# Eight-sequence decoder layer: the first norm turned by a transposing transfer, and products moved across the border of an iteration

## The chip, the cores and the metric

The kernel runs on one core of a Trainium2 chip. TensorE (PE) multiplies and turns 128 by 128 blocks, VectorE (DVE), ScalarE (ACT) and GpSimd (POOL) do elementwise work, and SyncE (SP) issues every transfer. The time is the device time of one execution in microseconds (us). Three executions of the kernel before are known, and one more with a profile.

## The reference

For 8 sequences of 512 rows by 256 columns, one pre-norm decoder layer:

```python
# x, ctx: (8, 512, 256)
x = x + attn(layernorm(x))
x = x + xattn(layernorm(x), ctx, ctx)
x = x + ffn(layernorm(x))

def attn(x):                       # 16 heads of 16 columns
    z = softmax(x @ W_A.T / 4, axis=rows)          # one weight per row and head
    roll[h, i, j] = z[h, i - j] if j <= i else 0   # a lower Toeplitz matrix per head
    return concat_h(roll[h] @ (x @ W_V.T)[:, h]) @ W_O.T + b_O

def xattn(q, k, v):                # one head of 256, causal
    return softmax(causal((q @ WQ) @ (k @ WK).T / 16)) @ (v @ WV)

def ffn(x):                        # 2 shared experts (128 wide), 16 routed (64 wide), best 2
    comb = weights of the two best of softmax(x @ router_w), zero elsewhere
    return sum_shared(silu(x @ wg) * (x @ wu)) @ wd + sum_e(comb[e] * silu(x @ wg[e]) * (x @ wu[e]) @ wd[e])
```

## The kernel before, in words

Each product is made of three half-precision passes on halves "hi" and "lo" of both operands (`three_passes`, lines 140 to 142). So whatever is turned or produced in fp32 is split: ACT writes hi, DVE writes fp32 minus hi as lo.

The program is a software pipeline of ten iterations, 0 to 9. Iteration `it` does three stages on three sequences: the first norm, softmax and values of sequence `it` (flag `f`), the Toeplitz product, W_O, second norm and cross attention of `it - 1` (flag `m`), and the feed forward of `it - 2` (flag `d`). The flag `n` says that a sequence `it + 1` follows. Iterations 2 and 3 (`c` = 6, 7) also compute context products; 4, 5 and 6 are one loop body and are called the steady ones here; 7 has no `n`, 8 has no `f`, 9 has only `d`. The order on each engine is written out by hand, and semaphores join the engines.

On PE a steady iteration is: router logits (`rows<-w_r,h3T`), softmax product z (`score<-h1T,w_a`), Toeplitz products (`wide<-val,toep`) with half the values (`rows<-w_v,h1T`), eight blocks of `mix` turned, the other values, `comb` turned, then ten gate and up products g0/u0 to g9/u9 (`score<-h3T,w_gu`, `rows<-h3T,w_gu`), each followed some steps later by its `down` (`wide<-w_d,mid`). Among them stand W_O (`rows<-w_o,mixT`), the turned `h2`, the scores, probabilities and attention. After u9 come down 7, eight blocks of `h3` turned, down 8, eight blocks of `h1` of the next sequence turned, down 9. The stretch between down 9 of one iteration and the Toeplitz products of the next is called the border. Turned blocks go to the two PSUM banks `turned`, from which ACT and DVE split them to `h1T`, `h2T`, `h3T`, `mixT` (`part_turned`, lines 630 and 819).

On DVE every gate j is `open_gate` (line 878, and line 884 with the router weights that a transfer repeats over partitions: `comb_rows`, in the tile `stage`) and `pass_gate` (line 892). ACT runs the tanh of a gate (line 678) and the hi part of `mid` (683), POOL the lo part (536). `normalise` is line 809. POOL takes the square root of a variance (528, 531) and adds the bias: `x_bo = x_in + b_o` (543), in a steady iteration just behind mid 1. The Toeplitz matrices of a sequence are loaded from a scratch in memory (`toep`, 2 x 2 MB), `x_in` with 512 KB per sequence.

`wide` is both the sum of the down products and the result of the Toeplitz products, so the latter wait until DVE has moved the sum into `x_out` (line 1069, two instructions, one signal).

## Time and profile before

| | |
|---|---|
| median of 3 runs | 645.68 us (642.64 to 646.45) |
| profiled execution | 646.66 us |
| its span in the trace | 644.9 us |
| mean granted TensorE clock | 0.974 of full speed |
| a steady iteration | 66.5 us |

The span is what the trace shows from the first to the last instruction; the profiled execution's own time holds 1.8 us more, which lie around it.

### The profile page before, as it was taken

How to read it: one execution, taken by the hardware profiler on the slowest of the kernel's cores; microseconds unless marked ns; L12 is line 12 of the kernel's file. 1: busy time of each engine (PE TensorE's matmuls, PEld its weight loads, DVE VectorE, ACT ScalarE, POOL GpSimd, SP SyncE). 2: the span in 40 equal slices, each digit the busy share in tenths (PEclk: the TensorE clock that was granted, in tenths of full speed). 3: DMA queues.
4: the chain of work that ended last, by engine and by line, in shares of the span. 5: the costliest groups of instructions: out<-in, count | busy, mean ns of one | idle time of the engine just before them, and what ended most of it. 6: DMA issues, size and time to landing. Idle time of an engine off the chain costs nothing. (4 is left out here: it accounts for less than half of the span.)

```text
span 644.9 us, 13750 instructions
## 1 busy us (share of the span) xinstructions
PE 578.3 (90%) x5212; PEld 388.5 (60%) x5212; DVE 459.1 (71%) x1137; ACT 224.2 (35%) x450; POOL 195.1 (30%) x221
## 2 busy tenths in 40 slices
PE   2768697989999999999999999999989979997696
PEld 1446365755686566766685667666855666664354
DVE  4485567676976788777877797779786866687363
ACT  3564343434243333333333333332423322322121
POOL 4314230332422322243324242414242312132122
PEclk9979789999999999999999999999999998999899
DMA  7884924296116901292119411951186105000600
GB/s 246 284 268 149 343 78 183 76 277 211 67 35 150 343 4 66 79 291 93 67 45 277 138 65 37 240 183 65 37 183 212 67 34 134 1 1 34 132 2 34
DMA packets 61249, 84.26 MB, mean 131 GB/s; under 512 B 2832, under 2 KB 46736, under 8 KB 60944
## 3 DMA queue, kind: packets, MB, share of 16 engines
q1 hardware_dynamic: 61200, 83.60, 43.6%
q8 instruction: 32, 0.52, 0.4%
q14 instruction: 17, 0.14, 0.1%
HBM read 71.47 MB, written 12.12 MB: 130 GB/s over the span
## 5 line engine op out<-in xcount | busy, mean ns | idle before, releaser
L536 POOL TENSOR_TENSOR mid<-gated,mid 128x512 f16<-128x512 f32 x80 | 93.4, 1167 | 233.3 <-ACT mid L683 233.3
L683 ACT ACTIVATE mid<-gated 128x512 f16<-128x512 f32 x80 | 50.1, 627 | 125.6 <-DVEq L895 125.6
L140 PE MATMUL wide<-w_d,mid 128*128 128x256 f16 x320 | 87.9, 275 | 3.5 <-POOL mid L536 3.5
L878 DVE SCALAR_TENSOR_TENSOR gated<-gated,score 128x512 f32<-128x512 f32 x80 | 54.3, 679 | 47.3 <-ACT gated L678 47.3
L141 PE MATMUL wide<-w_d,mid 128*128 128x256 f16 x320 | 87.8, 274 | 0.0
L142 PE MATMUL wide<-w_d,mid 128*128 128x256 f16 x320 | 87.8, 274 | 0.0
L140 PE MATMUL score<-h3T,w_gu 128*128 128x512 f16 x160 | 61.3, 383 | 5.0 <-DVEq L120 3.5
L678 ACT ACTIVATE gated<-score 128x512 f32<-128x512 f32 x80 | 47.2, 590 | 47.5 <-PE score L142 42.6
L140 PE MATMUL rows<-h3T,w_gu 128*128 128x512 f16 x160 | 60.9, 381 | 1.2 <-DVEq L120 1.2
L141 PE MATMUL score<-h3T,w_gu 128*128 128x512 f16 x160 | 61.1, 382 | 0.0
L142 PE MATMUL score<-h3T,w_gu 128*128 128x512 f16 x160 | 61.1, 382 | 0.0
L141 PE MATMUL rows<-h3T,w_gu 128*128 128x512 f16 x160 | 60.9, 380 | 0.0
L142 PE MATMUL rows<-h3T,w_gu 128*128 128x512 f16 x160 | 60.6, 379 | 0.0
L892 DVE SCALAR_TENSOR_TENSOR gated<-gated,rows 128x512 f32<-128x512 f32 x80 | 54.9, 686 | 4.5 <-DVE gated L884 1.0
L884 DVE TENSOR_TENSOR gated<-gated,stage 128x512 f32<-128x512 f32 x64 | 51.0, 797 | 6.8 <-DMA stage<-comb_scratch 4.3
L1099 PE MATMUL turned<-ident,h 128*128 128x128 f32 x192 | 28.4, 292 | 26.3 <-DVE h L809 16.4
L665 ACT ACTIVATE prob<-score,s_bias 128x128 f32<-128x128 f32 (+3 forms) x32 | 16.9, 528 | 78.7 <-DVE s_bias L845 78.7
L140 PE MATMUL wide<-val,toep 128*128 128x64 f16 (+3 forms) x512 | 41.2, 180 | 2.6 <-DVE x_out L1069 1.0
L140 PEld LDWEIGHTS wide<-val,toep 128*128 128x128 f16 x512 | 40.3, 96 | 5.1 <-issue 2.3
L809 DVE TENSOR_SCALAR h<-x_res,mean_var,rstd 128x256 f32<-128x256 f32 x64 | 39.3, 675 | 4.5 <-POOL rstd L531 2.7
L1099 PEld LDWEIGHTS turned<-ident,h 128*128 128x128 f32 x192 | 22.0, 148 | 33.9 <-issue 22.4
L141 PE MATMUL wide<-val,toep 128*128 128x64 f16 (+3 forms) x512 | 41.1, 180 | 0.2 <-issue 0.2
(193 smaller groups left out, 1384.6 us busy)
## 6 DMA issues: line engine op xcount, KB each, us to landing
toep<-z_scratch SPq DMA_DIRECT2D x16, 2048.0 KB, 16.2
stage<-comb_scratch SPq DMA_DIRECT2D x32, 512.0 KB, 8.0
x_in<-in_x SPq DMA_DIRECT2D x8, 512.0 KB, 10.8
out<-x_out SPq DMA_DIRECT2D x8, 512.0 KB, 3.0
qT<-q_scratch SPq DMA_DIRECT2D x7, 512.0 KB, 3.8
vx<-v_scratch SPq DMA_DIRECT2D x7, 512.0 KB, 5.0
q_scratch<-stage SPq DMA_DIRECT2D x6, 512.0 KB, 5.6
v_scratch<-stage SPq DMA_DIRECT2D x6, 512.0 KB, 6.1
```

Of the source, the lines that this page charges most:

```text
L140: pe.matmul(out, stationary[0], moving[0], start=start, stop=False, **kw)
L141: pe.matmul(out, stationary[0], moving[1], start=False, stop=False, **kw)
L142: return pe.matmul(out, stationary[1], moving[0], start=False, stop=stop, **kw)
L536: pool.tensor_tensor(mid[:, 1, j % SLOTS], gated[:, j % SLOTS], mid[:, 0, j % SLOTS], ALU.subtract).then_inc(mid_split.sem, 1)
L665: act.activation(prob[:, c % 2, 0:n], score.bank(f"s{c}")[:, 0:n], ACT.Exp, bias=s_bias[:, c:c + 1], scale=1 / (X_Q * X_H), accum_out=s_su ...
L678: act.activation(gated[:, j % SLOTS], score.bank(f"g{j}")[:], ACT.Tanh, scale=0.5 / (X_H * X_W)).then_inc(tanh_done.sem, 1)
L683: act.activation(mid[:, 0, j % SLOTS], gated[:, j % SLOTS], ACT.Copy).then_inc(mid_hi.sem, 1)
L809: last = dve.tensor_scalar(dst[:, c], src[:, c], mean_var[n][:, c, 0:1], rstd[n][:, c:c + 1], ALU.subtract, ALU.mult)
L878: dve.scalar_tensor_tensor(to, to, 1.0, score.bank(f"g{j}")[:], ALU.add, ALU.mult).then_inc(score.taken.sem, 1)
L884: dve.tensor_tensor(to, to, comb_rows[:, j - NSH], ALU.mult).then_inc(opened.sem, 1)
L892: dve.scalar_tensor_tensor(to, to, X_MID / (2 * (X_H * X_W) ** 2), rows.bank(f"u{j}")[:], ALU.mult, ALU.mult).then_inc(rows.taken.sem, 1)
L1099: last = pe.transpose(turned.bank(f"{use}.{k}")[:, P * c:P * c + P], src[:, c, P * k:P * k + P], ident[:])
```

## The change

1. `h1` of sequences 3 to 7 is no longer turned by PE. `x_in` is loaded from `xr`, a copy of x whose rows run backwards within blocks of 128, and is normalised in place. ACT and DVE split it unturned into `h1p` (hi and lo, 128 x 1024 each), and one transposing DMA of SP writes `h1T`. Sequences 0 to 2 are still turned by PE.
2. At the end of iterations 2 to 6, PE does: u9, h3 turned, down 7, z of the next sequence, down 8, its logits, down 9. The next iteration then begins with the first half of the values, and only then come the Toeplitz products, whose second half waits for the second half of `x_out` alone.
3. `comb` is turned behind g0/u0 and taken by DVE behind gate 0, where both stood ahead of these.
4. `x_bo` is loaded by a transfer of its own (512 KB), and the bias is added in place on POOL at gate 5 instead of gate 1.
5. On DVE, the statistics of the next `x_in` go to gates 3 and 4, its normalisation to gate 5, the new split to gate 6; the third norm stands between opening and passing gate 8; `probT` is split between opening and passing a gate. `h2` and `h3` signal by halves, and PE turns them block row by block row (`turn_halves`).
6. The Toeplitz results lie in `wide` in row order, so that ACT's copy of them (now into `h2`) is no longer permuted.

The core of the diff:

```diff
+            def move_h1(b):
+
+                sp.wait_ge(rows.ready.sem, rows.is_ready(b - 1, "v2"))
+                hold(sp, h1p_split, h1p_split.at(b - 3, 1))
+                sp.dma_start(h1T[:].rearrange("p a k (c s) -> p (a k c) s", s=P),
+                             h1p[:].rearrange("p a k c e -> p (a k c e)"), transpose=True).then_inc(h1T_moved.sem, 16)
...
+                if d and n:
+                    load_x(it + 1, 1 if c == 6 else None)
+                if f and d:
+                    load_residual(it)
...
                 if f and m:
                     fetch_context(it, it)
-                if d:
-                    sp.wait_ge(y_taken.sem, y_taken.at(it - 2, 1))
+                if n and d:
+                    move_h1(it + 1)
+                if d:
+                    sp.wait_ge(y_taken.sem, y_taken.at(it - 2, 2))
...
+            def part_h1(b):
+
+                dve.wait_ge(h1p_hi.sem, h1p_hi.at(b - 3, 1))
+                hi, lo = (h1p[:, a].rearrange("p k c e -> p c k e") for a in range(2))
+                dve.tensor_tensor(lo, x_in[:].rearrange("p c (k e) -> p c k e", k=K2), hi,
+                                  ALU.subtract).then_inc(h1p_split.sem, 1)
...
                 for j in range(AHEAD, MID):
                     if d:
-                        gate(it, it - 2, j)
+                        open_gate(it, it - 2, j)
+                    if m and j == AHEAD + C + 1:
+                        normalise(it - 1, it, 2, x_res, h3)
+                    at = j - AHEAD
+                    if m and at < C:
+                        part_prob(it, it - 1, at)
+                    if d:
+                        pass_gate(it, it - 2, j)
...
-                        if j == 5:
+                        if d and j in (3, 4):
+                            x_statistics(it + 1, range(2 * (j - 3), 2 * (j - 3) + 2))
+                        if first and j == 5:
                             x_statistics(it + 1)
-                        if j == C + AHEAD:
-                            normalise(it + 1, it, 0, x_in, h1)
+                        if j == (5 if d else C + AHEAD):
+                            normalise(it + 1, it, 0, x_in, x_in)
+                        if d and j == 6:
+                            part_h1(it + 1)
...
+            def turn_halves(it, use, src, made, b):
+
+                pe.wait_ge(turned.taken.sem, turned.is_free(it, f"{use}.1"))
+                turned.fill(pe, it, f"{use}.0")
+                turned.reached[(id(pe), True)] = turned.order.index(f"{use}.1") + 1
+                for c in range(C):
+                    if c % 2 == 0:
+                        pe.wait_ge(made.sem, made.at(b, c // 2 + 1))
+                    for k in range(K2):
+                        last = pe.transpose(turned.bank(f"{use}.{k}")[:, P * c:P * c + P], src[:, c, P * k:P * k + P],
+                                            ident[:])
+                        if c == C - 1:
+                            last.then_inc(turned.ready.sem, 1)
...
-                if m:
-                    pe.wait_ge(h_ready[2].sem, h_ready[2].at(it - 1, 1))
-                    turn(it, "h3", h3)
+
+                if d and not m:
+                    down(it - 2, MID - 3)
+                if m:
+                    turn_halves(it, "h3", h3, h_ready[2], it - 1)
+                if d and m:
+                    down(it - 2, MID - 3)
+                if n and d:
+                    score.reach(pe, score.ready, it)
+                    pe.wait_ge(h1T_moved.sem, h1T_moved.at(it - 2, 16))
+                    z_product(it + 1)
+                elif n:
+                    pe.wait_ge(h_ready[0].sem, h_ready[0].at(it + 1, 2))
+                    turn(it, "h1", x_in)
                 if d:
                     down(it - 2, MID - 2)
-                if n:
-                    pe.wait_ge(h_ready[0].sem, h_ready[0].at(it + 1, 1))
-                    turn(it, "h1", h1)
+                if n and d:
+                    turned.reach(pe, turned.ready, it)
+                    rows.reach(pe, rows.ready, it)
+                    logits(it + 1)
                 if d:
                     down(it - 2, MID - 1)
```

How the instructions stand, on VectorE at the end of the loop body (`L878`/`L926` and `L884`/`L932` open a gate, `L892`/`L940` pass it). Before, from gate 7 to the end:

```order
L878 SCALAR_TENSOR_TENSOR gated<-gated,score0 128x512
L884 TENSOR_TENSOR gated<-gated,stage 128x512
L892 SCALAR_TENSOR_TENSOR gated<-gated,rows0 128x512
...
L800 BN_AGGR mean_var2<-stats2 128x2 x4
...
L809 TENSOR_SCALAR h1<-x_in,mean_var0,rstd0 128x256 x4
...
L878 SCALAR_TENSOR_TENSOR gated<-gated,score1 128x512
...
L884 TENSOR_TENSOR gated<-gated,stage 128x512
L892 SCALAR_TENSOR_TENSOR gated<-gated,rows1 128x512
...
L809 TENSOR_SCALAR h3<-x_res,mean_var2,rstd2 128x256 x4
```

And now, from the new split at gate 6:

```order
L859 TENSOR_TENSOR h1p<-x_in,h1p 128x4x2x128
...
L926 SCALAR_TENSOR_TENSOR gated<-gated,score0 128x512
...
L932 TENSOR_TENSOR gated<-gated,stage 128x512
L940 SCALAR_TENSOR_TENSOR gated<-gated,rows0 128x512
...
L833 BN_AGGR mean_var2<-stats2 128x2 x4
...
L926 SCALAR_TENSOR_TENSOR gated<-gated,score1 128x512
...
L932 TENSOR_TENSOR gated<-gated,stage 128x512
...
L842 TENSOR_SCALAR h3<-x_res,mean_var2,rstd2 128x256 x4
L940 SCALAR_TENSOR_TENSOR gated<-gated,rows1 128x512
```

The first norm has left gate 7 (it stands at gate 5), a split of 128 x 1024 has come in at gate 6, and the third norm stands ahead of passing gate 8.

On GpSimd, the middle of the loop body from mid 4 on, now:

```order
L551 TENSOR_SCALAR var_eps<-mean_var 128x4
L554 TENSOR_TENSOR rstd<-var_eps,minus_half 128x4
...
L559 TENSOR_TENSOR mid<-gated,mid 128x512
...
L567 TENSOR_TENSOR x_bo<-x_bo,b_o 128x256 x4
...
L559 TENSOR_TENSOR mid<-gated,mid 128x512
L551 TENSOR_SCALAR var_eps<-mean_var 128x4
L554 TENSOR_TENSOR rstd<-var_eps,minus_half 128x4
```

The four bias additions stand between mid 5 and mid 6; before, they stood behind mid 1, beside the second norm.

On SyncE, the end of the loop body, now:

```order
L415 DMA x_in<-in_xr 128x4x256
...
L421 DMA x_bo<-in_x 128x4x256
...
L496 DMA toep<-z_scratch 128x16x512
...
L447 DMA qT<-q_scratch 128x2048
L448 DMA vx<-v_scratch 128x2048
...
L427 DMA_TRANSPOSE h1T<-h1p 128x16x128
...
L521 DMA out<-x_out 128x4x256
```

The transposing transfer stands behind the two context loads and ahead of the output; the loads of `x_in` and `x_bo` stand ahead of the Toeplitz loads, where `x_in` stood behind them.

## Rows read from the trace of the kernel before

**Rows 1.** The page: busy time of the engines, share of the span, instructions.

```profile
PE 578.3 (90%) x5212; PEld 388.5 (60%) x5212; DVE 459.1 (71%) x1137; ACT 224.2 (35%) x450; POOL 195.1 (30%) x221
```

**Rows 2.** Busy time by window (us, PE, PEld, DVE, ACT, POOL, clock, DMA).

```profile
390.40:457.00 66.60, 64.58 (x616) 44.11 (x614) 52.62 (x136) 23.03 (x48) 22.05 (x24) 1.00 0.45 127
...
522.70:589.50 66.80, 63.16 (x581) 42.57 (x582) 46.79 (x119) 20.27 (x42) 15.09 (x15) 0.95 0.16 41
...
430.50:450.00 19.50, 18.75 (x123) 11.63 (x120) 18.03 (x42) 5.53 (x10) 7.83 (x9) 1.00 0.15 54
```

**Rows 3.** Timeline of PE, iteration 6 (start, us, what, idle before).

```profile
411.94 1.09 PE L1099 MATMUL turned<-ident,h 128*128 128x128 f32 x8 [0.22 <-DVE h L809]
...
414.95 0.23 PE L140 MATMUL score<-h2T,qT 128*128 128x128 f16 x1 [0.61 <-DVE h2T L819]
...
448.05 0.27 PE L140 MATMUL wide<-w_d,mid 128*128 128x256 f16 x1
...
450.02 1.09 PE L1099 MATMUL turned<-ident,h 128*128 128x128 f32 x8 [0.50 <-DVE h L809]
450.95 0.27 PE L140 MATMUL wide<-w_d,mid 128*128 128x256 f16 x1
...
452.84 1.25 PE L1099 MATMUL turned<-ident,h 128*128 128x128 f32 x8 [0.42 <-DVE h3T L819]
453.94 0.28 PE L140 MATMUL wide<-w_d,mid 128*128 128x256 f16 x1
...
455.27 0.17 PE L140 MATMUL rows<-w_r,h3T 128*128 128x16 f16 x1
```

**Rows 4.** Timeline of DVE, the same iteration.

```profile
412.61 1.09 DVE L884 TENSOR_TENSOR gated<-gated,stage 128x512 f32<-128x512 f32 x1
...
439.43 0.67 DVE L878 SCALAR_TENSOR_TENSOR gated<-gated,score 128x512 f32<-128x512 f32 x1
...
443.39 1.35 DVE L809 TENSOR_SCALAR h<-x_in,mean_var,rstd 128x256 f32<-128x256 f32 x4
...
445.37 1.26 DVE L884 TENSOR_TENSOR gated<-gated,stage 128x512 f32<-128x512 f32 x1
446.67 0.69 DVE L892 SCALAR_TENSOR_TENSOR gated<-gated,rows 128x512 f32<-128x512 f32 x1
447.67 2.22 DVE L809 TENSOR_SCALAR h<-x_res,mean_var,rstd 128x256 f32<-128x256 f32 x4 [0.31 <-DVE gated L892]
```

**Rows 5.** Timeline of SP and POOL, the same iteration.

```profile
403.06 2.56 SPq L461 DMA_DIRECT2D stage<-comb_scratch  x4
...
410.96 3.32 POOL L543 TENSOR_TENSOR x_bo<-x_in,b_o 128x256 f32<-128x256 f32 x4
...
448.16 1.26 POOL L536 TENSOR_TENSOR mid<-gated,mid 128x512 f16<-128x512 f32 x1 [2.07 <-ACT mid L683]
```

**Rows 6.** Groups of DVE by form (busy, mean ns, idle before).

```profile
L792 DVE BATCH_NORM_STATS2 stats<-x_in 128x6 f32<-128x256 f32 x32 | 11.1, 410 | 6.3 <-DMA x_in<-in_x 6.3
...
L780 DVE SCALAR_TENSOR_TENSOR w_gu<-stage,w_gu 128x1024 f16<-128x1024 f32 x4 | 4.8, 1217 | 0.3 <-ACT w_gu L617 0.3
```

**Rows 7.** DMA issues (KB each, median us to landing); then line 410 (`x_in`) by itself.

```profile
stage<-comb_scratch SPq DMA_DIRECT2D x32, 512.0 KB, 8.0
...
out<-x_out SPq DMA_DIRECT2D x8, 512.0 KB, 3.0
...
DMA to landing us min/median/max: 3.7/10.8/13.6
```

**Rows 8.** Timeline of PE, waits in iterations 7 to 9 (second norm, down 9, Toeplitz).

```profile
479.14 1.09 PE L1099 MATMUL turned<-ident,h 128*128 128x128 f32 x8 [0.97 <-DVE h L809]
...
519.83 0.28 PE L140 MATMUL wide<-w_d,mid 128*128 128x256 f16 x1 [1.27 <-POOL mid L536]
...
522.86 0.19 PE L140 MATMUL wide<-val,toep 128*128 128x64 f16 x1 [0.96 <-DVE x_out L1069]
```

**Rows 9.** Timeline of DVE in iteration 1, the second norm.

```profile
66.17 2.93 DVE L809 TENSOR_SCALAR h<-x_res,mean_var,rstd 128x256 f32<-128x256 f32 x4
```

More of the change, by code:

```diff
@@ L583, in iteration @@
                     reciprocal_deviation(it - 1, 1)
-                if first:
-                    pool.wait_ge(rows.taken.sem, rows.is_taken(it, "o2"))
-                    add_bias(it)
                 for j in range(MID):
@@ L1060, in iteration @@
                         banks.reach(dve, banks.taken, it)
+                else:
+                    rows.reach(dve, rows.taken, it)
                 if m:
                     part_turned(it, it - 1, h3T, h3T_hi, "h3")
-                if n:
-                    part_turned(it, it + 1, h1T, h1T_hi, "h1", reverse=True)
+                if n and d:
+                    score.reach(dve, score.taken, it)
+                    z_max(it + 1)
+                elif n:
+                    part_turned(it, it + 1, h1T, h1T_hi, "h1")
+                for banks in (turned, score) if d and not n else (turned,):
+                    banks.reach(dve, banks.taken, it)
                 if d:
@@ L1068, in iteration @@
                     for g in range(2):
[L1069 removed]
+                        dve.scalar_tensor_tensor(
                             x_out[:, 2 * g:2 * g + 2], wide[:, g].rearrange("p (c e) -> p c e", c=2),
[L1071 to L1074 removed]
+                            1 / (X_MID * X_W), x_out[:, 2 * g:2 * g + 2], ALU.mult, ALU.add).then_inc(y_taken.sem, 1)
             x_statistics(0)
             part_weights(range(2))
[L1078 removed]
+            normalise(0, -1, 0, x_in, x_in)
             part_weights(range(2, EARLY))
[L1080 removed]
+            part_turned(-1, 0, h1T, h1T_hi, "h1")
             turned.reach(dve, turned.taken, -1)
@@ L1133, in context, with logits, z_product @@
                     last.then_inc(ctx_ready.sem, 1)
+            def logits(it):
+                rows.fill(pe, it, "logit")
+                pe.wait_ge(turned.taken.sem, turned.is_taken(it - 1, "h3.1"))
+                for q in range(C):
+                    for k in range(K2):
+                        last = three_passes(pe, rows.bank("logit")[:, NE * q:NE * q + NE],
+                                            parts(h3T, k, slice(P * q, P * q + P)), parts(w_r, k, slice(None)),
+                                            start=(k == 0), stop=(k == K2 - 1))
+                last.then_inc(rows.ready.sem, 1)
+            def z_product(b):
+                score.fill(pe, b, "z")
+                for k in range(K2):
+                    last = three_passes(pe, score.bank("z")[0:H, :], parts(w_a, k, slice(None)),
+                                        parts(h1T, k, slice(None)), start=(k == 0), stop=(k == K2 - 1))
+                last.then_inc(score.ready.sem, 1)
             def toeplitz(it, b, g):
@@ L1307, in iteration @@
                     context(1, range(UNITS))
-                for banks in (turned, score, rows):
-                    banks.reach(pe, banks.ready, it)
-            pe.wait_ge(h_ready[0].sem, h_ready[0].at(0, 1))
-            turn(-1, "h1", h1)
+                if not (n and d):
+                    for banks in (turned, rows, score):
+                        banks.reach(pe, banks.ready, it)
+            pe.wait_ge(h_ready[0].sem, h_ready[0].at(0, 2))
+            turn(-1, "h1", x_in)
             turned.reach(pe, turned.ready, -1)
```

199 lines of the change are left out of this document (104 added, 95 removed).

## The prediction

> **What bounds the kernel now.** I read the page first. PE is busy for 90% of the span, DVE for 71%, and ACT and POOL for a third [rows 1]. Then the windows by iteration: in a steady one PE is busy for 64.58 of 66.60 us at the full clock [rows 2], so PE's list of work is the time, and only two things can shorten it: work taken off PE, and the 2.0 us in which it stands still. The timeline of PE shows where it stands: 0.22 us ahead of the turned `h2`, 0.61 ahead of the scores, 0.50 ahead of the turned `h3` and 0.42 ahead of the turned `h1` [rows 3]. The reader should see that each of these names DVE. DVE is busy for 18.03 of 19.50 us between gates 5 and 8 [rows 2]: an engine with 71% over all has nearly nothing free just ahead of the border, and that is where this change adds to it.
>
> **h1 is no longer turned by PE (iterations 2 to 6).** Down 8 starts at 450.95 and down 9 at 453.94 [rows 3]. A down lasts 1.33 us on PE (453.94 to 455.27, where the logits start [rows 3]), so the turned `h1` with its wait costs 453.94 - 450.95 - 1.33 = 1.66 us. With z and logits between the downs instead, which are only moved, PE has work while `h3T` is split. Gain 1.66 an iteration, 8.3 in five.
>
> **h3 is turned ahead of down 7, not behind it.** Before, down 7 started at 448.05 and hid 1.33 us of the wait; both were done at 450.95 [rows 3]. Now PE wants `h3` at 448.05, and the question is when DVE has it; before it was complete at 447.67 + 2.22 = 449.9 [rows 4]. DVE's list up to there changes thus:
> - two statistics and the aggregation stand at gate 4; what idle time they find there I put at half of their 1.2 us: 0.6 later;
> - four statistics (4 x 0.41 [rows 6]) and 0.3 for the aggregation leave gate 5: 1.9 earlier;
> - the new split is 128 x 1024; the nearest row, the same shape with two inputs and an fp16 result, took 1.22 us [rows 6]: 1.2 later, and up to 1.8 if POOL's mid 6 runs beside it. In these rows an opened gate took 1.26 beside a mid and passing it 0.69, and a norm 2.22 beside a mid and 1.35 without [rows 4, 5]. I take 1.5;
> - the first norm itself is only moved, from 7 to 5, but now beside mid 5 or the bias additions: 0 to 0.9 later, by the same two norms; I take 0.5;
> - gate 6 is opened beside the bias additions (before, gate 2 was: 1.09 us [rows 4]): 0.4 later;
> - the third norm stands ahead of passing gate 8, which saves 0.69 and the 0.31 idle ahead of the norm [rows 4]: 1.0 earlier;
> - gate 8's opening may lose its mid beside it: 0 to 0.6 earlier; I take 0.3.
>
> That sums to 0.6 - 1.9 + 1.5 + 0.5 + 0.4 - 1.0 - 0.3 = -0.2, so `h3` is complete at 449.7. Half of its blocks are turned by then, the rest takes some 0.45 us, and down 7 ends at 451.5 where it was 450.95: a loss of 0.5. With the kind ends of the list PE does not wait at all (0.93 + 1.33 from 448.05, 450.3: a gain of 0.6), with the unkind ones `h3` comes at 450.7 and the loss is 1.5.
>
> **The second norm and the start of an iteration.** The bias additions lasted 3.32 us from 410.96 [rows 5], beside the second norm; with them gone to gate 5, the 0.22 idle ahead of the turned `h2` goes, and with the halves the overlap too. But both banks of the turned `h2` are now complete only at the end, so ACT starts later, and behind it stands the wait for the scores of 0.61 [rows 3]. A second limit comes nearer: the router weights are issued at 403.06 [rows 5] and take 8.0 us to land [rows 7], 411.1, and gate 2 used them at 412.61 [rows 4]: 1.5 us of slack. After down 9 nothing is moved for them (logits go ahead, but `comb` waits for g0 and u0), while gate 2 comes earlier by the z and logits moved across the border, some 2 us. So they come some 0.5 late, and the copies of `h2T` stand behind them on DVE. Gain 0.4 an iteration, between 0 (the weights eat it) and 1.0 (both waits and the overlap go). The values put ahead of the Toeplitz products hide the first `x_out`, which z and logits hid before: nothing either way; if that cover were missing it would cost what iteration 8 shows, 0.96 [rows 8].
>
> **Other iterations.** Iteration 7 waited 0.97 for the second norm [rows 8]: gain 1.0. At its end and at that of iteration 8, down 9 waited 1.27 for its mid [rows 8]; passing gate 8 is later but the third norm earlier and the tanh of gate 9 stands ahead of a copy, so I take half, 0.7 each. Iteration 8's Toeplitz products waited 0.96 for both halves of `x_out` [rows 8] and now for one: 0.7. In iteration 1 the second norm took 2.93 beside the bias [rows 9] instead of 1.35, and of these 1.6 I take 1.0. Together 4.1.
>
> **Costs at nothing.** The extra 512 KB for `x_bo` and 512 KB for the transposing transfer go to a queue that keeps the DMA engines 45% busy [rows 2]; `x_bo` is wanted 40 us after its load. The load waits on SP for W_O's result, and the Toeplitz loads queue behind it; they are wanted at the next border, so they have some 40 us too. ACT's split of `h1p` replaces its two copies of `h1T`. Toeplitz results in row order change no size.
>
> **The transposing transfer** is seen nowhere in this trace. DVE came to gate 7 at 439.43 [rows 4]; with the list above up to the split and the first norm's 1.35 (ahead of it now, at gate 7 before) it ends near 441.5 to 442, and z wants `h1T` at 451.5: 9.5 us. The nearest rows are the other 512 KB transfers: 3.0 us for the output and 3.7 to 13.6 (median 10.8) for `x_in`, which queues behind 4 MB of Toeplitz loads [rows 7]. The transposing one has 1 MB of context ahead of it; I take 5 us, within its cover.
>
> **Sum.** 5 x (1.66 - 0.5 + 0.4) + 4.1 = 11.9 us. The profiled execution took 646.66 (span 644.9), 1.0 above the median of the three runs, 645.68. So 634.8 in such an execution, and 633.8 as the median.
>
> **Rivals.**
> - *PE never waits.* The kind ends: 5 x (1.66 + 0.6 + 1.0) + 4.1 = 20.4, so 625; for it speaks that the norm is now signalled by halves; against it DVE's full window.
> - *DVE is the bound ahead of the border.* The unkind ends: 5 x (1.66 - 1.5) + 4.1 = 4.9, so 641, which is no change by the measure below.
> - *The clock.* Iteration 8 ran at 0.95 of the clock behind waits of 1.27 and 0.96 [rows 2, 8], 3.3 us lost of 66.8. A wait of over 1.5 us in one piece at `h3` could do this in five iterations: 633.8 + 5 x 3.3 = 650. Against it: steady iterations with four waits of up to 0.61 kept 1.00 [rows 2, 3], and only one of the four would grow.
> - *The transfer is late* (the other side). z cannot start, and down 8, logits and down 9 are queued behind it on PE. It decides from 9.5 us, and from 9.5 + 11.9 / 5 = 11.9 us the whole is slower. With the slowest `x_in`, 13.6 us [rows 7], it is 4.1 late, 20.5 in five: 654. Against it: that row is one behind 4 MB.
>
> What the output's row shows is an ordinary transfer, 3.0 us. The Trainium skill is at odds with itself on a transposing one: Advanced Engine Details and Errata, X-Bar Transpose (TRN2), has it as fast as a regular DMA, while VectorE: DVE Perf Modes, The three transpose paths, gives 1309 ns for one 128 x 128 block, which for the 16 blocks here, one after another, is an estimate of 21 us: 11.5 late and a time of 691. No row here shows either. That rule would put this rival at its worst; I give it 3 of this rival's 13%.
>
> **How the numbers follow.** Forecast 50%, PE never waits 20%, DVE the bound 12%, clock 5%, transfer late 13%. About 1% (6.5 us) is what this kernel's measurement can tell from no change. Below 639.2 lie the first two and a part of the third: 0.74. Within: 0.12. Slower than 652.1: 0.14. The range takes in the second and third rivals up to their ends, 625 to 646; the late transfer, the clock and a rest of faster ones stay out. The likeliest case by itself: 629 to 639.
>
> **What would show it.** Right: no turned `h1` from iteration 3 on, between down 7 and down 9 of iterations 2 to 6 no wait of PE, a wait of 1 to 2 us ahead of the turned `h3`, steady iterations of 65.0 us, a second norm of 1.4 us. Wrong: a wait ahead of `score<-h1T` that ends with the transfer (its landing over 9.5 us), a wait of gate 2 for `comb_scratch` of over 1 us, PE's clock below 1.00 in windows of iterations 4 to 6, or a first and third norm that both take over 2 us.

## The result, and the profile of the changed kernel

| | before | changed |
|---|---|---|
| median, us (runs) | 645.40 (6) | 649.76 (6) |
| lowest to highest | 642.28 to 649.77 | 645.57 to 651.80 |
| profiled execution, us (span) | 646.66 (644.9) | 650.26 (648.4) |

The ratio is 1.0073, 95% interval 1.0043 to 1.0103: slower by 0.7%, where 633.8 us was forecast.

The page of the changed kernel, the line of busy times, which answers to [rows 1]:

```profile
PE 571.4 (88%) x5172; PEld 383.8 (59%) x5172; DVE 465.4 (72%) x1132; ACT 222.4 (34%) x445; POOL 195.1 (30%) x221
```

PE has 6.9 us less to do and is busy for a smaller share of a longer span. The windows of one steady iteration, from one turned `h3` to the next (us, then busy us of PE, PEld, DVE, ACT and POOL, PE's granted clock, the DMA engines' busy share and GB/s), and the gates 5 to 8, which answer to [rows 2]:

```profile
385.88:453.53 67.65, 63.28 (x606) 43.31 (x607) 54.14 (x136) 22.66 (x47) 21.61 (x24) 1.00 0.50 140
430.50:453.50 23.00, 20.89 (x130) 12.53 (x128) 20.56 (x43) 7.66 (x14) 9.95 (x12) 1.00 0.46 135
```

PE's work in an iteration fell from 64.58 to 63.28, but it stands still for 4.37 us where it was 2.0, and DVE is busy for 54.14 us where it was 52.62. The timeline of PE shows where it stands (start, us, what, idle before), against [rows 3]:

```profile
418.36 0.23 PE L140 MATMUL score<-h2T,qT 128*128 128x128 f16 x1 [1.55 <-DVE h2T L852]
...
453.53 0.52 PE L1170 MATMUL turned<-ident,h 128*128 128x128 f32 x3 [1.41 <-DVE h L842]
...
459.56 0.17 PE L140 MATMUL rows<-w_r,h3T 128*128 128x16 f16 x1 [0.69 <-DVE h3T L852]
```

The waits of 0.22 and 0.42 ahead of the turned `h2` and `h1` are gone; in their place stand 1.41 ahead of `h3` (0.50 before), 0.69 ahead of the logits, and 1.55 ahead of the scores (0.61 before; 2.08, 0.91, 1.55, 1.49 in iterations 4 to 7). Two smaller ones, 0.20 and 0.53 us ahead of the attended values (`turned<-vx,probT`), make up the rest of the 4.37; before, there was one of 0.26 in that stretch. DVE's timeline of the same iteration names the cause; it answers to [rows 4]:

```profile
416.41 0.69 DVE L932 TENSOR_TENSOR gated<-gated,stage 128x512 f32<-128x512 f32 x1 [1.44 <-DMA stage<-comb_scratch]
...
437.46 3.32 DVE L842 TENSOR_SCALAR x_in<-x_in,mean_var,rstd 128x256 f32<-128x256 f32 x4
440.71 0.68 DVE L926 SCALAR_TENSOR_TENSOR gated<-gated,score 128x512 f32<-128x512 f32 x1
...
444.29 2.05 DVE L859 TENSOR_TENSOR h1p<-x_in,h1p 128x1024 f16<-128x1024 f32 x1
...
451.90 2.13 DVE L842 TENSOR_SCALAR h<-x_res,mean_var,rstd 128x256 f32<-128x256 f32 x4 [0.31 <-POOL rstd L554]
...
455.58 1.55 DVE L932 TENSOR_TENSOR gated<-gated,stage 128x512 f32<-128x512 f32 x1
```

And POOL's, which answers to [rows 5]:

```profile
437.28 1.16 POOL L559 TENSOR_TENSOR mid<-gated,mid 128x512 f16<-128x512 f32 x1 [1.60 <-ACT mid L706]
438.39 2.98 POOL L567 TENSOR_TENSOR x_bo<-x_bo,b_o 128x256 f32<-128x256 f32 x4
444.10 1.16 POOL L559 TENSOR_TENSOR mid<-gated,mid 128x512 f16<-128x512 f32 x1 [2.73 <-ACT mid L706]
450.50 0.20 POOL L551 TENSOR_SCALAR var_eps<-mean_var 128x4 f32<-128x4 f32 x1 [5.24 <-DVE mean_var L833]
450.77 1.02 POOL L554 TENSOR_TENSOR rstd<-var_eps,minus_half 128x4 f32<-128x4 f32 x1
451.77 1.15 POOL L559 TENSOR_TENSOR mid<-gated,mid 128x512 f16<-128x512 f32 x1
455.43 1.16 POOL L559 TENSOR_TENSOR mid<-gated,mid 128x512 f16<-128x512 f32 x1 [2.51 <-ACT mid L706]
```

The reader should lay the two side by side. Each operation of DVE that takes longer than it does elsewhere has one of POOL beside it, and the single instructions end at POOL's end plus about their own length. Gate 9's opening starts at 455.58, POOL's mid runs to 456.59, the opening ends at 457.13, 0.54 later; alone it takes 0.69. The split starts at 444.29, mid 6 ends at 445.26, the split 1.08 later. The first norm (four instructions; 1.35 us before [rows 4], where POOL did only the 128 x 4 root of a variance beside it) has mid 5 and four bias additions beside it and takes 3.32. The fused operations with one input in PSUM, as `L926` at 440.71, take their 0.68 although the additions run to 441.37. So DVE waits here, and the profile calls it busy. That is a reading of the timelines so far; bias_last, best1, mid_first and spread test it.

The transposing transfer, by its line (its rows on SP's queue):

```profile
L427 SPq DMA_TRANSPOSE h1T<-h1p x5: 3428/3531/4513, 170.3 to 446.4; - x5
DMA to landing us min/median/max: 5.2/6.4/6.9
```

The last starts at 446.43; z, which waits for it, starts at 455.99, straight behind down 7, so PE never stood for it.

### The profile page after: what moved, and what is told of

Its sections match the earlier page's. It is cut to its first block and busy times, and to the rows that moved or that the text cites. A ratio compares the mean times of both kernels' runs of the same rounds, so it can differ in the third digit from the quotient of the medians.

```text
span 648.4 us, 13665 instructions
## 1 busy us (share of the span) xinstructions
PE 571.4 (88%) x5172; PEld 383.8 (59%) x5172; DVE 465.4 (72%) x1132; ACT 222.4 (34%) x445; POOL 195.1 (30%) x221
## 5 line engine op out<-in xcount | busy, mean ns | idle before, releaser
L926 DVE SCALAR_TENSOR_TENSOR gated<-gated,score 128x512 f32<-128x512 f32 x80 | 54.2, 677 | 40.0 <-ACT gated L701 38.7
L932 DVE TENSOR_TENSOR gated<-gated,stage 128x512 f32<-128x512 f32 x64 | 53.3, 834 | 12.7 <-DMA stage<-comb_scratch 10.7
L940 DVE SCALAR_TENSOR_TENSOR gated<-gated,rows 128x512 f32<-128x512 f32 x80 | 54.5, 681 | 1.8
L140 PE MATMUL wide<-val,toep 128*128 128x64 f16 (+3 forms) x512 | 41.0, 180 | 1.3 <-DVE probT L884 0.9
L140 PEld LDWEIGHTS wide<-val,toep 128*128 128x128 f16 x512 | 40.5, 96 | 1.9 <-DVE probT L884 1.4
L141 PE MATMUL wide<-val,toep 128*128 128x64 f16 (+3 forms) x512 | 40.9, 180 | 0.0
L142 PE MATMUL wide<-val,toep 128*128 128x64 f16 (+3 forms) x512 | 40.9, 180 | 0.0
L141 PEld LDWEIGHTS wide<-val,toep 128*128 128x128 f16 x512 | 40.4, 96 | 0.1
L142 PEld LDWEIGHTS wide<-val,toep 128*128 128x128 f16 x512 | 40.3, 96 | 0.0
## 6 DMA issues: line engine op xcount, KB each, us to landing
x_bo<-in_x SPq DMA_DIRECT2D x8, 512.0 KB, 11.9
```

Source lines behind the costliest of these rows:

```text
L140: pe.matmul(out, stationary[0], moving[0], start=start, stop=False, **kw)
L141: pe.matmul(out, stationary[0], moving[1], start=False, stop=False, **kw)
L142: return pe.matmul(out, stationary[1], moving[0], start=False, stop=stop, **kw)
L926: dve.scalar_tensor_tensor(to, to, 1.0, score.bank(f"g{j}")[:], ALU.add, ALU.mult).then_inc(score.taken.sem, 1)
L932: dve.tensor_tensor(to, to, comb_rows[:, j - NSH], ALU.mult).then_inc(opened.sem, 1)
L940: dve.scalar_tensor_tensor(to, to, X_MID / (2 * (X_H * X_W) ** 2), rows.bank(f"u{j}")[:], ALU.mult, ALU.mult).then_inc(rows.taken.sem, 1)
```

## Experiments

The theories after the result: **A**, DVE's queue ahead of the border sets the time, above all where POOL works beside it; **B**, the router weights come late; **C**, PE lost the cover of down 7 when `h3` was turned ahead of it; **D**, the added transfers.

The ratios are each to the kernel before, executed beside the run. Its median was 645.47 us beside the first four runs, 644.58 beside comb_mid, norm_late and best1, 645.46 beside mid_first, spread and before_mid, and 645.36 beside the last two, so a difference between medians of two such groups can be off by up to 0.9 us.

**comb_early.** The weights' turning back in its old place.

```diff
-                if d:
-                    gate_up(it, 0)
-                if d and m and f:
-                    turn_comb(it)
+                if d and m:
+                    turn_comb(it)
+                if d:
+                    gate_up(it, 0)
```

(on DVE, `take_comb` likewise ahead of gate 0)

> The changed kernel, with one part undone: PE turns the router weights ahead of the first gate's products g0 and u0 again, and DVE copies them ahead of gate 0, so that SP issues their loads some 5 us earlier in an iteration. Everything else as in the changed kernel, whose steady iterations last 67.0 to 67.7 us. Theory A (the router weights come late: gate 2 waited 1.44 us for them in iteration 6, and the scores stood behind that with waits of 0.91 to 2.08 us in iterations 4 to 7): the wait of gate 2 goes, the scores wait 0.6 at most as before the change, and four iterations gain 0.5 to 1.4 us each: 3 to 5 us, about 645 to 647. Theory B (DVE ahead of the border is the whole loss): what is gained at the scores is lost again at the turned h3, whose wait grows from 1.42 us by as much; no change, 649 to 650. Theory C (the added transfers, 6.8 MB, slow the chain from z to x_out and the comb loads): the loads land later than 8 us behind their issue wherever they stand; below 1 us gained. Under A the wait ahead of the turned h3 stays at about 1.4 us.

Measured 649.37 us, ratio to before 1.0064 (1.0034 to 1.0093): no gain. Its PE timeline says why:

```profile
403.69 0.38 PE L1280 MATMUL turned<-ident,comb 128*16 128x128 f32 x2 [1.07 <-DVE mixT L852]
...
418.76 0.23 PE L140 MATMUL score<-h2T,qT 128*128 128x128 f16 x1 [0.59 <-DVE h2T L852]
```

The scores' wait is back at 0.59, as A of the expectation had it, and the wait ahead of `h3` stayed at 1.41, so the expectation's B did not happen either. What came was neither: PE wants the bank of the turned weights while DVE still copies `mixT`, and stands for 1.07 us. One wait had taken the place of the other.

**bias_last.** POOL's bias additions from gate 5 to behind mid 9.

```diff
-                    if f and j == (5 if d else 3):
+                    if f and j == (MID - 1 if d else 3):
                         add_bias(it)
```

> The changed kernel with one edit: POOL's bias additions (2.98 us in iteration 6) stand behind mid 9 at the end of the iteration and no longer at gate 5, where they ran beside DVE's first norm, which took 3.32 us (1.35 before the change, with nothing beside it). Theory A (DVE's list ahead of the border is the bound, and POOL beside it makes it longer): the first norm takes 1.4 to 2.2 us, the third norm and with it the turned h3 come some 1 to 2 us earlier, the wait of 1.42 us ahead of the turned h3 in iterations 4 to 6 falls to 0 to 0.6; 5 x 1.0 = 5 us, about 645. The second norm of the next iteration must not meet the additions: they start behind mid 9 and end some 3 us later, beside the copies of h3T. Theory B (the aggregation or the scores' chain sets the third norm, not the time of the first norm): DVE idles ahead of the third norm, no change. Theory C (the additions are late at their new place): DVE waits for x_biased ahead of x_res, and the time grows by 1 us an iteration.

Measured 641.63, ratio 0.9943 (0.9917 to 0.9969): 8.1 us less than the changed kernel by one line on an engine that is busy for 30%. DVE's first norm, which has only mid 5 beside it now (POOL, 429.14 to 430.30):

```profile
429.33 2.09 DVE L842 TENSOR_SCALAR x_in<-x_in,mean_var,rstd 128x256 f32<-128x256 f32 x4
```

3.32 has become 2.09, the wait ahead of `h3` fell from 1.41 to 0.85, and the 0.20 and 0.53 ahead of the attended values went. Not all of the 8.1 is the edit's: from the scores of iteration 2 to the turned `h3` of iteration 6 the traces give 304.77 us for 311.14, so 6.4. Another 3.0 of the 9.1 between the two spans lie ahead of those scores, where the two kernels do the same work, but the granted clock was 1.00 for 0.86 between the Toeplitz products and the turned `h2` of iteration 1.

**no_split.** The split taken out; the low half of the turned first norm is left out from iteration 3 on.

```diff
-                dve.tensor_tensor(lo, x_in[:].rearrange("p c (k e) -> p c k e", k=K2), hi,
-                                  ALU.subtract).then_inc(h1p_split.sem, 1)
+                dve.memset(lo[:, 0, 0, 0:2], 0.0).then_inc(h1p_split.sem, 1)
```

> The changed kernel without DVE's split of the turned first norm: the low half of h1p is set to zero once, and a write of 128 x 2 elements stands in an iteration where the 128 x 1024 subtraction stood (2.05 us in iteration 6). It leaves out the low half of h1T from iteration 3 on, so the values and z are less exact. It prices the split. Theory A (DVE ahead of the border is the bound): the third norm comes 1.5 to 2 us earlier, the wait of 1.42 us ahead of the turned h3 goes in four iterations, and 5 x 1.4 = 7 us less: about 643; if it is only a part of the queue that is long enough, 5 x 0.7, 646. Theory B (PE's own list and the clock set the time, DVE is not the bound): no change, 649 to 650.

Measured 638.61, ratio 0.9897 (0.9873 to 0.9922): 11.1 us less, more than A's 7. An operation of 2.05 us off DVE took 2.2 us an iteration off the whole by the medians, and 1.8 by the traces (268.87 us for 276.11 from the logits of iteration 2 to those of iteration 6). PE could follow nearly all of it, so DVE bounds this stretch.

**down7_first.** PE turns `h3` behind down 7 again, as before the change.

```diff
-                if m:
-                    turn_halves(it, "h3", h3, h_ready[2], it - 1)
                 if d and m:
                     down(it - 2, MID - 3)
+                if m:
+                    turn_halves(it, "h3", h3, h_ready[2], it - 1)
```

> The changed kernel with PE's order ahead of the turned h3 as it was before the change: down 7 first (1.33 us), then the turned h3 (1.42 us waited in iteration 6). Theory A (DVE ahead of the border is the bound for both orders: the second half of the third norm arrives when it arrives): PE waits some 0.1 instead of 1.4 us for the first half, but turning, down 8 and z stand behind down 7; the third norm's first half is ready at the same time as before, so the turned h3 starts at the same time and down 7, 1.33 us, no longer stands behind it: the gain is at most 1.33 us an iteration, and it arises only if what follows (z, down 8, logits, which wait 0.69 us for h3T on DVE and ACT) is not itself bound by DVE. If DVE's copies of h3T are the bound, the logits' wait grows from 0.69 to 2.0 us and nothing is gained: 649 to 650. Theory B (the lost cover of down 7 is a cost of its own): 5 x 1.0 = 5 us less, 645.

Measured 649.64, ratio 1.0054 (1.0028 to 1.0080): nothing, so C falls. Its PE waits:

```profile
451.41 0.28 PE L140 MATMUL wide<-w_d,mid 128*128 128x256 f16 x1 [0.85 <-POOL mid L559]
...
454.03 0.38 PE L140 MATMUL score<-h1T,w_a 128*16 128x512 f16 x1 [0.27 <-DVE gated L926]
...
457.99 0.17 PE L140 MATMUL rows<-w_r,h3T 128*128 128x16 f16 x1 [1.08 <-DVE h3T L852]
```

0.85 + 0.27 + 1.08 = 2.20 against 1.41 + 0.69 = 2.10. Down 7 is no cover, as its own mid stands on POOL behind the root of the third norm's variance.

**comb_mid.** On bias_last: the weights turned between g0 and u0; and in iteration 9 ACT's copy for mid 8 ahead of the tanh of gate 9, as before the change. The first edit on PE:

```diff
-                    gate_up(it, 0)
-                if d and m and f:
-                    turn_comb(it)
+                    gate_up(it, 0, (lambda: turn_comb(it)) if m and f else None)
```

> The kernel with the bias additions at the end of the iteration (641.6 us, steady iterations 66.0 us), and with two more edits. PE turns the router weights between g0 and u0, not ahead of both (where it waited 1.07 us for DVE's copies of mixT) and not behind both (where gate 2 waited 1.07 us for their loads and the scores 0.97 to 2.22 us); DVE copies them ahead of gate 0. And in iteration 9, which has no attention, ACT copies mid 8 ahead of the tanh of gate 9 again. Theory A (the weights' lateness and the wait ahead of their turning are two ends of one choice, and g0's 1.3 us cover the 1.07): no wait ahead of the turned weights, the scores wait 0.6 us, iterations 4 to 7 are 0.4 to 1.6 us shorter: 4 us, and the last down waits 0.95 instead of 1.73: about 637. Theory B (DVE ahead of the border is again the bound, so that time won at the scores comes back at the turned h3, 0.86 now): at most 1 us less, 640 to 641.6.

Measured 637.43, ratio 0.9860 (0.9822 to 0.9898): 4.2 us less. In iterations 4 to 6 there is no wait ahead of the turned weights, 0.59 ahead of the scores, and 0.85 ahead of `h3` as in bias_last: theory B holds, once PE has g0 to do meanwhile. Of the 4.2, the last down's wait gives 0.8 (1.73 to 0.96).

**norm_late.** On bias_last: the third norm behind passing gate 8.

```diff
-                    if m and j == AHEAD + C + 1:
-                        normalise(it - 1, it, 2, x_res, h3)
...
+                        if at == C + 1:
+                            normalise(it - 1, it, 2, x_res, h3)
```

> The kernel with the bias additions at the end of the iteration (641.6 us) and the third norm behind the passing of gate 8, where it stood before the change. It prices one term of the forecast, 1.0 us an iteration for the third norm ahead of the passing (0.69 of the passing and 0.31 of waiting for POOL's rstd). Theory A (the norm is on the path and the term is right): the turned h3 starts 0.4 to 1.0 us later, the wait of 0.86 us ahead of it grows to 1.3 to 1.8, and five iterations cost 2 to 5 us: 644 to 646. Theory B (mid 8 and gate 9, which then come earlier, give it back: the second half of h3T and z wait for gate 8's and 9's score bank): no change, 641 to 642.

Measured 641.43, ratio 0.9929 (0.9902 to 0.9956), bias_last's within its uncertainty. The turned `h3` waits 0.85, as there, and its second half 0.77, where the logits waited 0.69. DVE's third norm and POOL's mid 7 and mid 8:

```profile
444.53 2.25 DVE L842 TENSOR_SCALAR h<-x_res,mean_var,rstd 128x256 f32<-128x256 f32 x4 [0.30 <-DVE gated L940]
```

```profile
443.67 1.16 POOL L559 TENSOR_TENSOR mid<-gated,mid 128x512 f16<-128x512 f32 x1
445.03 1.28 POOL L559 TENSOR_TENSOR mid<-gated,mid 128x512 f16<-128x512 f32 x1 [0.21 <-ACT mid L706]
```

The third norm, 0.7 us later in DVE's list, meets only the last 0.30 us of mid 7, where it had nearly all of it beside it in bias_last (2.13 us). So its first half comes quicker, and its second half meets mid 8. The place was worth nothing on bias_last, where mid 7 stood beside the earlier one and mid 8 beside the later one.

**best1.** On comb_mid: the split on POOL, behind mid 6 (`pool.tensor_tensor` in place of `dve.tensor_tensor`, and `if n and d and j == 6: part_h1(it + 1)` in POOL's loop in place of DVE's).

> The kernel of comb_mid, and DVE's split of the turned first norm (2.05 us, on DVE at gate 6) moved to POOL, which does it behind mid 6. Theory A (DVE's queue ahead of the border is the bound, not the operation as such): the third norm comes up to 1.9 us earlier, the wait ahead of the turned h3 is gone, and PE waits only for h3T ahead of the logits (0.69 us) and for h2T: 3 to 6 us below comb_mid, near the kernel without any split plus what comb_mid gives, 633 to 636. Theory B (POOL beside DVE makes DVE's operations longer, as the bias additions did to the first norm, 3.32 us against 2.09): a POOL split of some 2.3 to 3 us beside gates 6 and 7 makes these longer by 1 to 2 us, POOL's mid 7 and rstd come late, and the gain is below 1 us. Theory C (the transposing transfer then starts some 1.5 us later): z waits for it only if it lands behind 456 on the old scale, 4.4 us of slack; no wait.

Measured 638.21, ratio 0.9881 (0.9842 to 0.9920): not faster than comb_mid. Theory B of the expectation; DVE's and POOL's timelines:

```profile
435.03 2.62 DVE L934 TENSOR_TENSOR gated<-gated,stage 128x512 f32<-128x512 f32 x1
```

```profile
434.98 2.13 POOL L574 TENSOR_TENSOR h1p<-x_in,h1p 128x1024 f16<-128x1024 f32 x1
```

POOL started 0.05 us ahead and ran to 437.11; DVE's opening, 0.69 alone (line 934 in this kernel, `L932` in the others), ended 0.54 behind that. The work has left DVE and its time has stayed. This is the clearest row for the mechanism. The Trainium skill, SBUF — State Buffer, Who interferes with whom, has it as a rule: VectorE in a mode that uses both ports, or with two inputs in SBUF, and GpSimd reading SBUF take one shared pair in turn, and whoever issues first blocks the other for the whole instruction. For the large operations the traces agree: the opening (two inputs in SBUF) waits to the end of POOL's, `L926` (one in PSUM) keeps its 0.68. For POOL's small ones they do not: in the changed kernel the root of a variance (128 x 4, two inputs in SBUF) started ahead of an opening, and the opening kept its 0.69:

```profile
434.67 1.01 POOL L554 TENSOR_TENSOR rstd<-var_eps,minus_half 128x4 f32<-128x4 f32 x1
```

```profile
434.73 0.69 DVE L932 TENSOR_TENSOR gated<-gated,stage 128x512 f32<-128x512 f32 x1
```

The measurement decides: what counts here is beside which of POOL's large operations DVE stands. No run shows why the small one is free.

**mid_first.** On comb_mid, one number in POOL's loop: mid 7 ahead of the third norm's deviation, where POOL had stood idle for 5.2 us.

```diff
-                    if m and j == (8 if first else 6):
+                    if m and j == (8 if first else 7 if d else 6):
                         reciprocal_deviation(it - 1, 2)
```

> The kernel of comb_mid (637.4 us, steady iterations 65.5 us) with one edit in POOL's order: mid 7 ahead of the third norm's reciprocal deviation, not behind it. POOL stood idle 5.2 us ahead of the deviation, and then ran mid 7 (1.16 us) just when DVE ran the third norm (2.13 us; the same operation took 1.35 where POOL was idle). DVE's list is untouched. Theory A (POOL's and DVE's operations on SBUF do not run side by side, DVE waits until POOL's has ended): mid 7 ends about when the aggregation does, the third norm takes 1.35 us and ends 0.7 to 0.8 us earlier, the wait of 0.86 ahead of the turned h3 falls by as much, and gate 9's opening may still meet mid 8 (1.55): 3 to 4 us less in five iterations, 633.5 to 634.5. Theory B (the longer norm has another cause, its place in DVE's queue or its four parts): norm and time unchanged, 637. Theory C (mid 7 ahead delays the deviation): the norm waits over 1 us, the time grows by 2 to 5 us.

Measured 633.41, ratio 0.9804 (0.9777 to 0.9832), 0.1 below the 633.5 to 634.5 of theory A. POOL and then DVE:

```profile
435.95 1.16 POOL L559 TENSOR_TENSOR mid<-gated,mid 128x512 f16<-128x512 f32 x1 [3.92 <-ACT mid L706]
437.26 0.19 POOL L551 TENSOR_SCALAR var_eps<-mean_var 128x4 f32<-128x4 f32 x1 [0.16 <-DVE mean_var L833]
```

```profile
438.65 1.38 DVE L842 TENSOR_SCALAR h<-x_res,mean_var,rstd 128x256 f32<-128x256 f32 x4 [0.29 <-POOL rstd L554]
```

DVE's list is that of comb_mid, its third norm takes 1.38 for 2.13, and the wait ahead of `h3` is gone.

**spread.** On mid_first: DVE's first norm between opening and passing gate 6, the split directly behind passing it.

```diff
+                    if n and m and d and j == 6:
+                        normalise(it + 1, it, 0, x_in, x_in)
                     at = j - AHEAD
...
                         pass_gate(it, it - 2, j)
+                    if n and m and d and j == 6:
+                        part_h1(it + 1)
...
-                        if j == (5 if d else C + AHEAD):
+                        if not d and j == C + AHEAD:
                             normalise(it + 1, it, 0, x_in, x_in)
-                        if d and j == 6:
-                            part_h1(it + 1)
```

> The kernel of mid_first, and on DVE the first norm stands between opening and passing gate 6 (it stood behind gate 5, beside mid 5: 2.08 us) and the split directly behind passing gate 6 (it stood some 1 us later, beside mid 6: 2.05 us). The same operations, at places where POOL is idle by the rows. Theory A (as in mid_first): the first norm takes 1.35 and the split about 1.1 to 1.4 us, the third norm comes 1.2 to 1.7 us earlier than in mid_first, and PE has no wait ahead of the turned h3; what is left are 0.69 for h3T and 0.59 for h2T. As only what is left of the 0.86 can be won at the turned h3, and a part of the 0.69: 0 to 0.6 us an iteration, 631 to 634. Theory B (nothing but the length of DVE's queue counts and these two are not on it any more): as mid_first. The transposing transfer starts at about the same time as before and must not be waited for.

Measured 626.85, ratio 0.9711 (0.9685 to 0.9737): 6.6 us under mid_first, more than A's 0 to 3. An iteration is 1.28 shorter (64.70 before): the whole 0.69 ahead of the logits went, where A had a part of it, and PE's busy time fell from 63.12 to 62.62, which A had not. It beats both kernels. A steady iteration, from scores to scores, and DVE's and POOL's rows:

```profile
336.46:399.88 63.42, 62.62 (x606) 43.46 (x607) 50.79 (x136) 22.78 (x47) 21.90 (x24) 1.00 0.54 150
```

```profile
420.58 1.38 DVE L842 TENSOR_SCALAR x_in<-x_in,mean_var,rstd 128x256 f32<-128x256 f32 x4
...
423.30 1.23 DVE L859 TENSOR_TENSOR h1p<-x_in,h1p 128x1024 f16<-128x1024 f32 x1 [0.15 <-DVE gated L940]
```

```profile
423.95 1.60 POOL L559 TENSOR_TENSOR mid<-gated,mid 128x512 f16<-128x512 f32 x1 [3.97 <-ACT mid L706]
```

The norm takes 1.38 for 3.32 in the changed kernel, the split 1.23 for 2.05. Here DVE was first, and POOL's mid 6 takes 1.60 for 1.16: it works in both directions. DVE's 136 instructions are busy for 50.79 us an iteration, in the changed kernel 136 for 54.14: 3.35 us of its "busy" time were waits for POOL. All the added transfers are still there, and the router weights took 7.9 us to land in the changed kernel for 8.0 before, so D falls too.

**before_mid.** The kernel before the change with the two orders alone: mid 7 ahead of the deviation, the third norm ahead of passing gate 8.

```diff
-                        gate(it, it - 2, j)
+                        open_gate(it, it - 2, j)
+                    if m and j == AHEAD + C + 1:
+                        normalise(it - 1, it, 2, x_res, h3)
+                    if d:
+                        pass_gate(it, it - 2, j)
```

> The kernel before the change with the two small orders alone: on POOL mid 7 ahead of the third norm's reciprocal deviation, and on DVE the third norm between opening and passing gate 8 (it stood behind the passing, beside mid 8: 2.22 us). It tells what of the gain over the kernel before needs the change at all. Theory A (the turned first norm off PE is worth 1.66 us an iteration once DVE is out of the way): this kernel wins only its own waits, 0.50 ahead of the turned h3 and a part of 0.42 ahead of the turned h1, 2 to 4 us in five iterations: 641 to 643, and stays 7 to 10 us behind spread. Theory B (the change's parts are worth nothing, and all that was won comes from POOL's order): 637 or less, near spread.

Measured 642.78, ratio 0.9954 (0.9935 to 0.9973), as A had it. Its third norm takes 1.38 us and the wait ahead of `h3` is gone, but PE still turns `h1`, and waits 0.54 for it. So 16 us lie between this and spread. They are not all shown to need the change: the turned `h1` was priced at 5 x 1.66 = 8.3, but the kernel before was not run with the bias additions, the first norm and mid 8's copy at the places that spread gives them.

**comb_late.** spread with the weights turned behind g0 and u0, as the change has them (the diff of comb_mid undone).

> The kernel of spread (626.9 us, steady iterations 63.4 us, no wait of PE at the border) with the router weights turned behind g0 and u0 again, as the change has it, and copied behind gate 0. It prices the weights' lateness where DVE ahead of the border is no longer the bound. Theory A (the weights are late and it is a cost of its own): gate 2 waits over 1 us for them, the scores wait 1.0 to 2.2 us in place of 0.59 in iterations 4 to 7, and the time grows by 2 to 5 us, to 629 to 632. Theory B (the second norm's copies are what the scores wait for, whatever the weights do): no change.

Measured 630.39, ratio 0.9781 (0.9754 to 0.9809): 3.5 us slower than spread, as A had it. DVE and PE:

```profile
401.11 0.69 DVE L932 TENSOR_TENSOR gated<-gated,stage 128x512 f32<-128x512 f32 x1 [1.65 <-DMA stage<-comb_scratch]
```

```profile
403.06 0.23 PE L140 MATMUL score<-h2T,qT 128*128 128x128 f16 x1 [1.76 <-DVE h2T L852]
```

**u3_ahead.** spread with PE's u3 ahead of the scores, to cover the last 0.59 (in code, `gate_up(it, AHEAD, some=(0, 1))` ahead of `scores(it, 0)`, its other half where it was).

> The kernel of spread with PE's product u3 (1.3 us) ahead of the first scores, where in every iteration PE stands 0.59 to 0.64 us for the copies of h2T. Theory A (the wait is that of two copies behind the turned h2, and u3 covers it): the wait goes in iterations 3 to 8, 6 x 0.6 = 3.6 us less, about 623. Theory B (the scores stand on the path to the third norm, through row maximum, softmax and attention on DVE and ACT, and come 0.7 us later): the wait turns up ahead of the turned probabilities, the attended values or the turned h3, and the time is 626 to 628.

Measured 630.63, ratio 0.9766 (0.9741 to 0.9790): 3.8 us slower, worse than either theory.

```profile
404.39 0.39 PE L140 MATMUL score<-h3T,w_gu 128*128 128x512 f16 x1 [0.97 <-DVE s_rsum L902]
```

The wait is gone at the scores and stands, larger, ahead of g3, which needs the bank of the first scores. u3 had been the cover between the two. That is 0.38 us more an iteration (63.80 for 63.42), 2.7 in seven; another 1.5 stands in iteration 8 of the profiled execution, where the clock was 0.94 between its Toeplitz products and g3 and 1.00 in spread.

## Why the prediction was wrong

- **h1 off PE** (1.66): right. PE's work fell by 1.30 us an iteration, and the wait of 0.42 went.
- **The transposing transfer** (5 us, hidden): right, 5.2 to 6.9 us and never waited for, so the rival on the other side fell. The 21 us worked out from the Trainium skill, VectorE: DVE Perf Modes, The three transpose paths, did not come; the rule of Advanced Engine Details and Errata, X-Bar Transpose (TRN2), in the same skill (as fast as a regular DMA) is nearer, at twice the output's 3.0 us.
- **DVE's list ahead of h3** (-0.2, so `h3` at 449.7 and a loss of 0.5): the step that failed. The sum took the longer sizes beside POOL for accidents of up to 0.9 us. The first norm, put at +0.5 for its place "beside mid 5 or the bias additions" with the larger of two norms as its end, met both one after the other and grew by 1.97 (3.32 for 1.35); bias_last, which moves the additions away, gave back 8.1 us by the medians and 6.4 by the traces. The split was 2.05 for 1.5. The third norm's new place, -1.0, was worth nothing (norm_late, on bias_last). On the other side gate 6's opening took 0.69, not 0.4 more than that, and gate 8's lost its whole 0.57. Counted from the first scores, `h3` was complete after 34.9 us before and 35.7 now, where the list has 34.7. Two costs of the same kind stood in no term: gate 9's opening (1.55 for 0.69) ahead of the copies of `h3T`, and with it 0.69 ahead of the logits; and the 0.5 more ahead of the attended values.
- **Down 7 behind h3**: the term was 0.5 with PE's wait at 1 to 2 us; the wait was 1.41, but the order costs nothing (down7_first); the lateness is DVE's, in either order.
- **The router weights** (0.5 late, gain 0.4 an iteration with it): mis-sized. Gate 2 waited 1.44 for them, the scores up to 2.08; comb_late prices it at 3.5 us over four iterations, 0.9 each. The copies of `h2T` stood behind it, as the text had it.
- **The second norm** (1.4 us): it took 2.22 for 2.63. The text had the bias additions beside it, but it ran from 409.25 to 411.88 and they began at 410.96; mid 1 (from 409.75 to 411.00) was beside it, and stayed.
- **Other iterations** (4.1): the totals look nearly right in part, by luck. Iteration 1 (1.0): its second norm took 1.37 for 2.93, but the turned `h3` of iteration 2 came at 177.41 for 177.44. The changed kernel had been 3.8 us ahead when the Toeplitz products of iteration 1 started (43.78 for 47.61), which no term has, and lost as much up to the turned `h2` (25.25 us for 21.64), where the granted clock was 0.86 for 1.00. Iterations 7 and 8 (3.1): from the turned `h3` of iteration 6 to down 9 of iteration 8 it was 132.94 us for 136.56, so 3.6 less, but 3.7 of that lie between down 9 of iteration 7 and the scores of iteration 8, where the clock was 1.00 for 0.88. The waits gave little: 0.97 less ahead of the second norm and 0.60 less ahead of the Toeplitz products, but 0.83 and 0.33 more ahead of the scores, and 1.36 and 1.13 ahead of down 9 for 1.27 and 1.25. Iteration 9 took 61.9 for 58.3: the tanh of gate 9 ahead of mid 8's copy costs 0.8 there (0.95 to 1.73), where the text counted such an order a help, and the granted clock is 0.92 for 0.95 (0.52, the lower of its two levels for nearly all the time, between 607 and 617 us).

Summed by PE's timelines: from the turned `h3` of iteration 2 to that of iteration 6, 272.58 us before and 276.12 after, so +3.5 where 4 x 1.56 = 6.2 less was forecast; ahead of it and behind it 0, where the other 5.7 of the 11.9 was forecast. That is 15.4 us in the span; between forecast and median it was 16.0.

The rival "DVE is the bound ahead of the border" named the mechanism and had 12%; its price, 641, took each cost from one neighbour beside it. The clock rival's price, 650, is what was measured, but its reason did not come: a wait of 2.08 us in one piece stood in iteration 4, and from the scores of iteration 2 to those of iteration 7 every window is at 1.00. "PE never waits", 625, is what spread nearly shows (626.85, 63.4 us an iteration): the ceiling was right, and the change reaches it only when POOL's operations stand elsewhere. Two of the four signs of "wrong" came true: gate 2 waited over 1 us for the router weights, and the first and third norm both took over 2 us (3.32 and 2.13).

What stays open: what of the last 3.6 us of iteration 9 is the clock's, and whether the change has a part in where the clock falls. Beside falls that both profiled executions have, it fell in iteration 8 before, and ahead of the turned `h2` of iteration 1 after.

## What to carry to other kernels

The busy time of VectorE can hold its waits for GpSimd: lay the two timelines side by side, and look for operations whose end is the other engine's end plus a constant. When a list is moved on the bound engine, cost each step by what stands beside it at the new place on the other engine, all of it and not the worst single row seen; then move the cheap engine's work into its idle gaps (5.2 us here). And a wait that is traded for cover elsewhere (comb_early, u3_ahead) comes back at the next user of the same bank: the place in the middle is often the right one.

## What the runs showed of the hardware

- DVE's 128 x 512 operation with two inputs in SBUF took 0.69 us alone, 1.55 beside a 1.16 us POOL operation that had started ahead of it, and 2.62 beside one of 2.13; POOL's took 1.60 for 1.16 where DVE had started first. That moving work from DVE to POOL can give nothing back (best1), I had not expected.
- POOL's 128 x 4 operation of 1.01 us beside the same DVE operation cost it nothing (0.69), nor did it lengthen a norm (1.35 us before the change, 1.38 in spread with nothing beside it).
- A transposing transfer of 512 KB within SBUF took 5.2 to 6.9 us from issue to landing, and up to 8.6 in spread, 3.4 to 5.5 of it on SP's queue.
